# Earlier products of the last batch's rows with the weights, and a different order of the packed bytes

## What is computed

```python
masks = (adj[None] == rel_ids[:, None, None, None])      # only relation 1 occurs
h = einsum('rbnm,bmd->rbnd', masks, x)                   # sum of neighbours' rows
y = einsum('rbnd,rdo->bno', h, weight)
out = layernorm(x + y + bias)                            # over the last axis, no scale or offset
```

## Time and profile before

| | us |
|---|---|
| median of 3 runs (112.17 to 112.3) | 112.23 |
| the profiled execution | 112.52 |
| its span, first to last instruction | 110.7 |
| busy: PE, PE's weight loads | 99.9, 92.7 |
| busy: DVE, ACT, POOL | 84.2, 84.2, 73.6 |
| HBM read 37.81 MB, written 4.19 MB | 379 GB/s over the span |

### The profile page before, as it was taken

The page is one execution under the profiler, slowest core; times in us unless marked ns, Lnnn a source line. Parts: engine busy times, 40 slices in busy tenths (PEclk is TensorE's granted clock), DMA queues, the critical chain, the costliest instruction groups (busy, mean ns, idle before and its releaser), DMA issues.

```text
span 110.7 us, 3051 instructions
## 1 busy us (share of the span) xinstructions
PE 99.9 (90%) x1107; PEld 92.7 (84%) x1108; DVE 84.2 (76%) x251; ACT 84.2 (76%) x103; POOL 73.6 (66%) x137
## 2 busy tenths in 40 slices
PE   5939899989999999989999899999999999999800
PEld 5927899879999799978999699999999999999700
DVE  1035665479753999779986999799999997997880
ACT  3057969797919986699695995979797979786850
POOL 3000800780498959979997999599989953942880
PEclk9999999999999999999999999999999999999995
DMA  3999999999999999999999999999999999992044
GB/s 52 366 417 417 420 425 432 432 423 411 426 432 429 407 431 426 426 420 426 423 423 423 420 426 426 425 428 423 423 420 429 423 423 414 420 379 89 6 192 189
DMA packets 7792, 42.20 MB, mean 381 GB/s; under 512 B 865, under 2 KB 994, under 8 KB 4194
## 3 DMA queue, kind: packets, MB, share of 16 engines
q1 hardware_dynamic: 7632, 41.49, 90.6%
q10 hardware_dynamic: 146, 0.52, 1.2%
HBM read 37.81 MB, written 4.19 MB: 379 GB/s over the span
## 4 chain that ended last, share of the span: by engine, by line
PE 53%; DMA 21%; SPq 8%; DVE 6%; ACT 5%; issue 4%; DVEq 0%; ACTq 0%
PE h_ps L663 29%; DMA adj_sb<-adj 21%; PE ids_t L644 10%; PE y_ps L676 9%; ACT bytes_of L528 4%; SPq L384 4%; PE h_ps L720 3%; SPq L395 2%; DVE mask_t L845 2%; SPq L381 2%; PE spare L699 2%; ACT mask_t L574 1%; DVE h_all L825 1%; DVE stats L858 1%; DVE x_sb L908 1%
## 5 line engine op out<-in xcount | busy, mean ns | idle before, releaser
L528 ACT ACTIVATE bytes_of<-adj_sb,offset 128x2048 fp8e4<-128x2048 int32 x32 | 64.0, 2001 | 4.6 <-DMA adj_sb<-adj 4.5
L845 DVE TENSOR_SCALAR mask_t<-ids_t 128x1024 uint16<-128x1024 uint16 x62 | 40.3, 681 | 14.1 <-PE ids_t L632 12.1
L663 PE MATMUL h_ps<-mask_t,x_hi 128*128 128x256 bf16 (+1 forms) x232 | 29.3, 269 | 1.2 <-DVE mask_t L845 1.2
L663 PE MATMUL h_ps<-mask_t,x_lo 128*128 128x256 bf16 (+1 forms) x232 | 29.4, 269 | 0.2 <-DVE x_lo L913 0.2
L455 POOL TENSOR_TENSOR x_sb<-x_sb,bias_sb 128x1024 f32<-128x1024 f32 x8 | 19.0, 2374 | 9.6 <-ACT bias_sb L586 9.2
L494 POOL TENSOR_SCALAR x_sb<-x_sb,rstd,shift 128x128 f32<-128x128 f32 x55 | 24.0, 455 | 0.9
L663 PEld LDWEIGHTS h_ps<-mask_t,x_lo 128*128 128x128 f16 x232 | 21.9, 98 | 2.8 <-DVE x_lo L913 0.4
L663 PEld LDWEIGHTS h_ps<-mask_t,x_hi 128*128 128x128 f16 x232 | 21.0, 98 | 3.5 <-DVE mask_t L845 1.6
L446 POOL TENSOR_TENSOR x_lo<-x_sb,x_hi 128x1024 f16<-128x1024 f32 x6 | 12.9, 2144 | 7.0 <-ACT x_hi L541 6.6
L644 PE MATMUL ids_t<-ident,bytes_of 128*128 128x128 bf16 x192 | 16.0, 226 | 0.9 <-ACT bytes_of L528 0.9
L644 PEld LDWEIGHTS ids_t<-ident,bytes_of 128*128 128x128 bf16 x192 | 14.8, 148 | 1.9 <-ACT bytes_of L528 1.8
(11 more groups left out here) (81 smaller groups left out, 88.8 us busy)
## 6 DMA issues: line engine op xcount, KB each, us to landing
adj_sb<-adj SPq DMA_DIRECT2D x28, 1024.0 KB, 23.9
adj_sb<-adj SPq DMA_DIRECT2D x8, 512.0 KB, 8.3
x_sb<-x SPq DMA_DIRECT2D x7, 512.0 KB, 22.7
out<-x_sb SPq DMA_DIRECT2D x7, 512.0 KB, 21.7
x_sb<-x ACTq DMA_DIRECT2D x1, 512.0 KB, 5.9
out<-x_sb SPq DMA_DIRECT2D x2, 256.0 KB, 2.1
w_sb<-weight SPq DMA_DIRECT2D x1, 64.0 KB, 8.0
bias_row<-bias ACTq DMA_DIRECT2D x1, 0.5 KB
```

Of the source, the lines that this page charges most:

```text
L528: nc.scalar.activation(bytes_of[:, at % ROOM].rearrange("p n t -> p t n"), adj_sb[:, slot, 2 * k:2 * k + 2, :], ACT.Square, scale=SLOPE, b ...
L663: last = nc.tensor.matmul(h_ps[g.bank][:, to], part[:, g.b % 2, j, :], mask_t[:, g.b % 2, j, cols], start=(j == 0 and part is x_hi), stop= ...
L845: nc.vector.tensor_scalar(mask_t[:, b % 2, :, u * P:(u + 1) * P].bitcast(UINT16), ids_t[bank_of(turn)][:, :, :].bitcast(UINT16), 1 << bit, ...
```

## The change

Two things are changed, each in several places.

The bytes: `check` writes the same bytes with the column index split as (q, s), s from 0 to 7, in the order s, q. ACT now reads every eighth int32 of a unit in its innermost loop and writes 128 words side by side for each s. `transpose_pair` reads word after word.

z: the load of batch 7's `x` moves to ACT's queue, right behind batch 0's `x`. The weight's load moves up to the second place in SP's queue. The transposes of batch 7's `x`, their copies, the products with the weight and the splits all move from turns 3, 5 and 7 into the work on group 0. The transposes become a transpose instruction instead of a product with the identity. The second half uses bank `h_ps[1]` instead of a bank of `ids_t` and, later, `spare`. Group 1 writes `h_ps[1]` too, so PE waits for both halves of `z_lo` ahead of group 1's first products. DVE's row maxima of z move from turn 9 to turn 2.

```diff
-        bytes_of = sb("bytes_of", [P, ROOM, N, 2], FP8)
+        bytes_of = sb("bytes_of", [P, ROOM, J, P, 2], FP8)
...
+        def half_of_z(half):
+
+            return (spare[:, :, :], h_ps[1][:, :].rearrange("p (n d) -> p n d", d=D))[half]
...
             load_unit(0, 0)
+            sp.dma_start(w_sb[:, 0, :], weight[0]).then_inc(s_w, 16)
             for u in range(1, J):
                 load_unit(0, u)
-                if u == GU:
-                    sp.dma_start(w_sb[:, 0, :], weight[0]).then_inc(s_w, 16)
...
-                    if k == PAIRS - 1 and b == EARLY:
-
-                        load_x(B - 1)
...
-                nc.scalar.activation(bytes_of[:, at % ROOM].rearrange("p n t -> p t n"), adj_sb[:, slot, 2 * k:2 * k + 2, :],
+                nc.scalar.activation(bytes_of[:, at % ROOM].rearrange("p s q t -> p t s q"),
+                                     adj_sb[:, slot, 2 * k:2 * k + 2, :].rearrange("p t (q s) -> p t s q", s=J),
                                      ACT.Square, scale=SLOPE, bias=offset[:, 0:1], saturate=False,
...
+            act.dma_start(units_of(x_sb[:, B - 1], B - 1, 0, J), rows_of(x, B - 1, 0, J)).then_inc(s_x[B - 1], 16)
...
             check(0, 1)
+            split_z(0)
             check(0, 2)
+            split_z(1)
...
-                    if n == 0 and g.index in Z_TURNS:
-                        split_z(Z_TURNS.index(g.index))
...
-                if at == FIRST_PACKED + 1:
-
-                    pe.wait_ge(s_kept, 2)
-                words = bytes_of[:, at % ROOM].bitcast(BF16)[:, :, 0].rearrange("p (k q s) -> p k s q", q=P, s=step(b))
+                words = bytes_of[:, at % ROOM].bitcast(BF16)[:, :, :, 0]
                 for j in range(J):
-                    last = nc.tensor.transpose(bank[:, j, :], words[:, j // step(b), j % step(b), :], ident[:, :])
+                    last = nc.tensor.transpose(bank[:, j, :], words[:, j, :], ident[:, :])
...
+                    if g.index == 1 and units[0] == g.first:
+
+                        pe.wait_ge(s_zl, 2)
...
-                    last = nc.tensor.matmul(to[:, n, :], x_sb[:, B - 1, half * HALF + n, :], whole_ident[:, :],
-                                            start=True, stop=True)
+                    last = nc.tensor.transpose(half_of_z(half)[:, n, :], x_sb[:, B - 1, half * HALF + n, :],
+                                               whole_ident[:, :])
...
+            transpose_last_x(0)
+            transpose_last_x(1)
             transpose_unit(0, 2)
             for part in (x_hi, x_lo):
                 products(g, g.units[1:2], part)
             transpose_unit(0, 3)
+            weigh_last_x(0)
             transpose_unit(0, GU)
+            weigh_last_x(1)
             products(g, g.units[2:], x_hi)
...
-            for u in range(1, GU + 2):
+            mask_unit(0, 1)
+            keep_last_x(0)
+            keep_last_x(1)
+            for u in range(2, GU + 1):
                 mask_unit(0, u)
+            split_z(0)
             row_maxima(0)
+            mask_unit(0, GU + 1)
+            split_z(1)
```

More of the change, by code:

```diff
@@ L133, in loads_of @@
         return 16 * len([c for c in range(b % ADJ_SLOTS, b + 1, ADJ_SLOTS) if not alone(c, 2 * k)])
-    Z_TURNS = [5, 7]
     def pairs_checked_by(g):
@@ L565, in split_z @@
                 act.wait_ge(s_z, half + 1)
-                nc.scalar.activation(z_hi[:, half * HALF:(half + 1) * HALF], spare[:, :, :], ACT.Copy,
+                nc.scalar.activation(z_hi[:, half * HALF:(half + 1) * HALF], half_of_z(half), ACT.Copy,
                                      scale=0.5).then_inc(s_zh, 1)
@@ L670, in project @@
                 if g.index == 0:
-                    pe.wait_ge(s_w, 16)
                     pe.wait_ge(s_biased, 1)
@@ L695, in weigh_last_x @@
                 pe.wait_ge(s_kept, half + 1)
-                if half:
-                    pe.wait_ge(s_zl, half)
+                if half == 0:
+                    pe.wait_ge(s_w, 16)
                 for n in range(HALF):
-                    last = nc.tensor.matmul(spare[:, n, :], x_t[:, half, n * P:(n + 1) * P], w_sb[:, 0, :],
+                    last = nc.tensor.matmul(half_of_z(half)[:, n, :], x_t[:, half, n * P:(n + 1) * P], w_sb[:, 0, :],
                                             start=True, stop=True)
@@ L781, in _ @@
                 project(groups[g.index - 1])
[L782 to L786, removed]
-                    weigh_last_x(Z_TURNS.index(g.index))
                 step_by_two(g, g.units[2:], n.b, n.first // 2)
@@ L819, in keep_last_x @@
                 dve.wait_ge(s_turned, half + 1)
-                if half == 0:
-                    source = spare
-                else:
-                    source = ids_t[bank_of(turn_of(FIRST_PACKED // PAIRS, 2))]
-                    source = source[:, :, :].bitcast(FP32).rearrange("p j q -> p (j q)").rearrange("p (n d) -> p n d", d=D)
-                nc.vector.tensor_copy(x_t[:, half, :].rearrange("p (n d) -> p n d", d=D), source[:, :, :]).then_inc(s_kept, 1)
+                nc.vector.tensor_copy(x_t[:, half, :].rearrange("p (n d) -> p n d", d=D), half_of_z(half)).then_inc(s_kept, 1)
             def split_z(half):
@@ L829, in split_z @@
                 js = slice(half * HALF, (half + 1) * HALF)
-                nc.vector.scalar_tensor_tensor(out=z_lo[:, js], in0=spare[:, :, :], scalar=0.5, in1=z_hi[:, js],
+                nc.vector.scalar_tensor_tensor(out=z_lo[:, js], in0=half_of_z(half), scalar=0.5, in1=z_hi[:, js],
                                                op0=ALU.mult, op1=ALU.subtract).then_inc(s_zl, 1)
@@ L963, in _ @@
                 sum_rows(q)
-                if unit_no(n.b, n.first) == 2 * FIRST_PACKED:
-                    keep_last_x(0)
-                    keep_last_x(1)
                 mask_unit(n.b, n.units[0])
@@ L971, in _ @@
                     combine(sets[q.b], q, sets[q.b].units)
-                if g.index in Z_TURNS:
-                    split_z(Z_TURNS.index(g.index))
-                if g.index == Z_TURNS[-1] + 2:
+                if g.index == 2:
                     row_maxima_of_z()
```

## The result

The changed kernel takes **161.24 us** (median of 4 runs, 160.95 to 161.5), against 112.27 (112.17 to 112.33) for the kernel before on the same chip: a ratio of 1.436, interval 1.4335 to 1.439. It is 49 us slower. The forecast was 151.5 us; direction and mechanism held, and the time was 9.7 us short. The stated range, 109 to 175 us, held it too, but that range was wide enough for a faster kernel as well; the likeliest case by itself had 124 to 175. The profiled execution took 161.2 us, its span is 159.4.

What follows compares the result with a forecast made beforehand. Adjacency landings, then PE, bound the old kernel; ACT's checks would bound the changed one. First check at 9.0, 32 checks 120.6, between them 10.2, tail 10.2, 1.82 around, less 0.3: 151.5 us, range 109.0 to 175.

Steps and rivals of the forecast that it cites:

- the likeliest case: ACT's checks take 2.6 to 4.8 us and the kernel 124 to 175 us; chance 0.66.
- That ACT is the bound: ACT, at 8.1 us a turn against PE's 5.3, is the only bound from first check to last.
- The size of a check: ACT's check, read at a 32-byte step, goes from 2.00 to 3.77 us.
- method (c): Price of ACT's check: PE's four-byte weight loads stream at ACT's 0.87 ns, so the step costs x2.0, 3.77 us.
- (a): Price of ACT's check if PE's four-byte load streams twice as long as the two-byte one: x1.53, 2.94 us.
- (b): Price of ACT's check if PE's four-byte load streams four times as long as the two-byte one: x2.6, 4.83 us.
- The tail: From the last check to the span's end, mask, last units, statistics and store stay at 10.2 us.
- z's part: Early-stage z work makes PE up to 1.8 us late at pair 8, won back by turn 11.
- Rival (1): The step is free on ACT, a check stays at 1.99 us, the kernel takes 109.7 us; chance 0.22.
- The wait for `z_lo`: PE's new wait ahead of group 1's products, put at 0 to 0.3 us and covered.
- Rival (2): ACT pays and PE's clock falls to half, turns of 10.6 us, 175 us in all; chance 0.07.
- Rival (3): Both free, z's move gives nothing, PE 3 us late at pair 8, 112.2 us; 0.05 together with a mild step.

Runs made afterwards that it cites:

- experiment 5: Early z alone, with ACT reading side by side and PE reading word after word, so masks are of other columns: 109.79 us, ratio 0.979.
- experiment 1: The changed kernel with the old byte order put back, leaving only z's early work: 110.17 us, in a second run 109.95 us (ratio 0.981).
- experiment 4: The kernel before with the new byte order alone, z left in turns 3, 5 and 7: 159.16 us, ratio 1.4215.
- experiment 6: Three kernels: the kernel before with other read or write orders in its first eight checks; read steps of 8 and 16 bytes took 2.18 and 4.21 us.
- experiment 2: The changed kernel with ACT reading side by side and writing each byte 256 bytes from the last: 325.25 us, ratio 2.905.

## Why the prediction was right, and where it was short

**That ACT is the bound, and that the step costs: right.** Forecast were ACT full from first check to last, PE's idle put down to ACT, loads of 98 ns (101, with the stretches at the lower clock in the mean) and no idle ahead of a split of z late in the kernel. All four are in the rows.

**The size of a check: the step that was short.** The prediction took 3.77 us, from a ratio of 2.0 on the 1.77 us of stream; measured were 4.05, that is (4.05 - 0.23) / 1.77 = 2.16. In the chosen method (c), PE's loads with ACT's pace in them, the shape of the argument was off as well as the number: it scaled the element, while the runs show a price per place visited. Its ratio came from 0.27 and 0.52 ns a word on PE, and ACT has 0.87 and 1.9, so that 2.0 lies so near 2.16 is in good part luck. What did carry over from PE's rows is that steps of 16 and of 32 bytes cost the same (148 ns both; on ACT 4.21 and 4.09 us). The neighbours (a) 2.94 and (b) 4.83 held the 4.05 between them. So did the estimate of 3.1 to 4.5 us from the Trainium skill's page Vector Engine (DVE) Microarchitecture Reference (5.2). Its upper end stands there for a step in both sources or in the destination, and not in one source alone, so the agreement says little. Of the 9.4 us that the sum is short, 8.8 are this one term. The sum, by its own terms, against the profiled 161.2 us where it had 151.8:

| term | forecast | measured | difference |
|---|---|---|---|
| first check begins | 9.0 | 9.07 | 0.1 |
| 32 checks | 120.6 | 129.4 | 8.8 |
| between them, 0.33 of waiting for PE included | 10.2 | 9.9 | -0.3 |
| from the last check's end to the span's end | 10.2 | 11.05 | 0.85 |
| sum, with 1.82 around it | 151.8 | 161.2 | 9.4 |

The profiled execution stands at the median this time (161.2 and 161.24), while the forecast took off 0.3; that gives the 9.7.

**The tail: 0.85 short.** It was held unchanged. In the kernel before, the mask of one unit and the root of the full set were under way or about to begin when pair 31's transposes came: the root began 0.15 us behind them (100.68 and 100.53). Now ACT comes out of its last check only then: mask at 148.31, root at 149.30, which is 0.81 behind PE's 148.49. DVE stood idle 2.96 us for that root, and its next mask stands behind it. So 0.7 of the 0.85 is ACT being late in the tail as well; the other 0.14 is the time from the check's end to PE's start, which the forecast had at zero.

**z's part: right in sum, wrong in two places.** Rival (1)'s price, both parts free, was 109.7 us; experiment 5, which is just that, took 109.79, and z alone 109.95. But PE was to be up to 1.8 us late at pair 8 and was 0.1 late: the early stage had idle time for nearly all the added work, and the transposes as an instruction are shorter than the products (below), which the forecast had left at "between nothing and 0.89". The wait for `z_lo` was put at 0 to 0.3 us. In the second run of experiment 1 it is 0.32:

```profile
18.84 1.03 PE L662 MATMUL h_ps<-mask_t,x_hi 128*128 128x256 bf16 x8 [0.32 <-DVE z_lo L817]
```

In the changed kernel it is 4.60, since `z_hi` of the second half stands on ACT behind checks of 4 us. It cost next to nothing, as ACT was the bound by then. The forecast of this wait fits the old check and not the longer one that the same forecast had.

**Rival (1), the step is free: fell.** By the Trainium skill's page ScalarE: Activation LUTs (What ACT_TABLE_LOAD costs) a check would have stayed at 1.99 us. The trace has 4.05 with a step of 32 bytes; the formula fits the checks side by side (1.99 to 2.01) and none with a step that costs.

**Rival (2), PE goes slow with it: half of it came, and its price fell.** The granted clock did fall twice to near its lower level, behind idle times of PE of 4.60 and 4.31 us. But it rose again, and stayed up while PE waited 1.1 to 1.8 us for every pair, so turns of 10.6 us never came to stay, and ACT felt 0.33 us. The end ran against 161, not 175.

**Rival (3), z gives nothing: fell** for z alone (2.4 us). In the changed kernel it is true, and more: the early `x` makes the change as a whole 2.1 us slower than the order of the bytes alone (experiment 4). That case was not among the rivals. Most of it is in the forecast's own term, the first check at 9.0 for 7.80: experiment 4's kernel begins it 1.54 us earlier.

The reading of why it costs, from the rows of experiment 6, with 0.23 us fixed: in reading, 2048 single visits take 3.98 us at 16 bytes and 3.86 at 32, so 1.9 ns each; over all steps of 16 bytes and more it is 1.8 to 1.9; two words at a time, 1024 visits take 1.99, again 1.94 ns each; four at a time, 512 visits would take 1.0 us and are hidden under the engine's own 0.87 ns x 2048 = 1.78. In writing, 512 visits of four bytes take 2.39 us, 1024 of two 4.78, and 2048 of one 8.84 to 9.27: 4.3 to 4.7 ns each. The order of the kernel before visits 256 places in writing, which by this is 1.2 us and hidden.

The Trainium skill's page Advanced Engine Details and Errata (SBUF Cachelines) has lines of 16 bytes and asks for at least two hits on each. For ACT's reading the trace agrees: two hits 2.18 and 2.22 us, one hit 3.9 to 4.2 (but 2.45 with two regions in turn). For ACT's writing of bytes it does not: two hits take 5.01 and even four 2.62, against 1.99.

**Open.** Why a write visit costs some 2.4 times a read visit, and why two regions in turn are cheap, no run shows. A layout that would leave ACT runs of two or four words was not tried; by experiment 5 there is little to be had from it, some 0.2 us.

## What to carry to other kernels

Before a step is moved from one engine to another, read two rows: what the engine that is relieved has on the path (here 0.2 us of PE's 1.2), and what margin the engine that will pay has in a turn (here 0.6 to 0.9 us on ACT, against 4.1 asked). Price a stepped operand of ACT by the number of 16-byte places that it visits, not by its elements or bytes: some 1.9 ns each in reading and 4.5 in writing, against the engine's own 0.87 ns per element, whichever is more. That is measured for int32 in and bytes out, 2048 elements, and does not hold for two regions read in turn. And take a bundle of edits apart: here one half gains 2% and the other loses 42%.

## What the runs showed of the hardware

- ACT with int32 in and bytes out: 2048 elements take 2.0 us side by side. Read at steps of 16, 32, 64, 128, 256, 512 and 1024 bytes they take 3.9 to 4.2, and at 8 bytes 2.18. Written at steps of 16, 32, 64, 256, 512 and 1024 bytes they take 9.1 to 9.5, at 8 bytes 5.0 and at 4 bytes 2.6. Two regions read in turn take 2.45.
- PE's weight load of 128 16-bit words takes 98 ns side by side and 148 at a step of 16 or 32 bytes. The pitch of its transposes differs only by 6 ns, 62 and 56: loads and products run side by side (busy for 84% and 90% of the same span).
- The float32 transposes as a transpose instruction: four follow each other within 0.50 and 0.43 us, where as products with the identity four took 0.89. These are three rows of PE's timeline of the changed kernel, where the third is what follows them:

```profile
10.63 0.66 PE L685 MATMUL spare<-whole_ident,x_sb 128*128 128x128 f32 x4
11.13 0.60 PE L685 MATMUL h_ps<-whole_ident,x_sb 128*128 128x128 f32 x4
11.56 0.67 PE L632 MATMUL ids_t<-ident,adj_sb 128*128 128x128 bf16 x8
```

- The granted clock fell to near its lower level behind two idle times of PE of over 4 us, and did not fall for the 21 waits of 1.1 to 1.8 us from 62 us on. In experiment 2, where PE waited 4.6 us a pair on average (110.0 us in 24 waits), the mean clock of the whole span was 0.666.
